# Attention's normed input, written by VectorE at the end of a step instead of by ScalarE at the start of the next

## The reference

```python
def _layernorm(x, axis=-1, eps=1e-05):
    m = jnp.mean(x, axis=axis, keepdims=True)
    v = jnp.var(x, axis=axis, keepdims=True)
    return (x - m) / jnp.sqrt(v + eps)
...
    h = _L0_tok_ref(x, ...)                        # out = einsum('bgcd,gbc->bcd', x, softmax weights)
    h = h + _L0_attn_ref(_layernorm(h, axis=-1), ...)
    h = h + _L0_ffn_ref(_layernorm(h, axis=-1), ...)
```

## Time and profile before

| | |
|---|---|
| median of 3 runs | 495.94 us (493.77 to 498.94) |
| profiled execution, its own time | 495.68 us |
| its span, first to last instruction | 493.5 us |
| PE busy | 428.6 us (87%) |
| DVE busy | 301.3 us (61%) |
| ACT busy | 250.2 us (51%) |
| POOL busy | 234.7 us (48%) |
| mean granted TensorE clock | 0.965 |

### The profile page before, as it was taken

How to read it: one execution, slowest core, us unless ns; L and a number is a source line. 1 busy time by engine, 2 the same in 40 slices (tenths; PEclk the granted TensorE clock), 3 DMA queues, 4 the chain that set the end, 5 groups by cost and what they waited for, 6 DMA issues and landing times.

```text
span 493.5 us, 13284 instructions
## 1 busy us (share of the span) xinstructions
PE 428.6 (87%) x3982; PEld 332.6 (67%) x3982; DVE 301.3 (61%) x1045; ACT 250.2 (51%) x708; POOL 234.7 (48%) x267
## 2 busy tenths in 40 slices
PE   1568889999999999766479999999999999978985
PEld 1546667777777777532368887888888888863654
DVE  3674678999899887875514344444443434341997
ACT  4165687887788876543025444444454544430000
POOL 1060003566556667667606556565665656560000
PEclk9989999999999999997679999999999999998998
DMA  8999990122122122222246596677677757635995
GB/s 265 344 352 263 291 278 30 68 80 86 68 75 69 66 77 89 80 83 94 101 131 209 161 294 204 182 237 215 187 237 216 244 139 218 213 132 208 405 393 211
DMA packets 56479, 90.01 MB, mean 182 GB/s; under 512 B 7720, under 2 KB 43691, under 8 KB 56401
## 3 DMA queue, kind: packets, MB, share of 16 engines
q1 hardware_dynamic: 44016, 61.69, 41.1%
q0 software_dynamic: 10080, 25.29, 14.5%
q10 hardware_dynamic: 2304, 2.10, 1.2%
HBM read 84.00 MB, written 40.82 MB: 253 GB/s over the span
## 4 chain that ended last, share of the span: by engine, by line
PE 35%; issue 7%; POOL 3%; DMA 2%; DVE 2%; SPq 1%; POOLq 0%; DVEq 0%
PE ps_low L1104 19%; PE ps L1104 11%; PE ps_low L1356 4%; POOL y_rows L449 3%; PE ps L1343 2%; DMA y_rows<-y,xring 1%; DMA xring<-slot_rows 1%; DVE x_sb L862 0%; DVE h_all L1087 0%; POOL slot_rows L420 0%; DVE x_sb L1099 0%; DVE x_sb L1092 0%; SPq L302 0%; SPq L352 0%; SPq L357 0%
## 5 line engine op out<-in xcount | busy, mean ns | idle before, releaser
L449 POOL DMA_INDIRECT y_rows<-y,xring x114 | 112.1, 983 | 90.1 <-issue 81.6
L1104 PE MATMUL ps_low<-wring,probt 128*128 x456 | 118.7, 383 | 0.0
L1065 DVE TENSOR_TENSOR probt<-probt,ps_low 128x128 f32<-128x128 f32 x114 | 32.8, 288 | 107.2 <-issue 92.6
L1104 PEld LDWEIGHTS ps_low<-wring,probt 128*128 128x128 f32 x456 | 78.6, 193 | 6.2
L1104 PE MATMUL ps<-wring,probt 128*128 x228 | 68.2, 382 | 0.0
L600 ACT COPY probt<-ps_low 128x256 f32<-128x256 f32 x115 | 42.8, 372 | 48.8 <-PE ps_low L1356 48.7
L605 ACT ACTIVATE probt<-ps_low 128x128 f32<-128x128 f32 x114 | 31.6, 277 | 57.3 <-PE ps_low L1104 57.3
L1058 DVE TENSOR_SCALAR y<-ps,xring 128x256 f32<-128x256 f32 x114 | 54.6, 479 | 7.2 <-DMA y_rows<-y,xring 6.0
L420 POOL DMA_INDIRECT slot_rows<-row,slot_ix x48 | 48.7, 1014 | 16.9 <-issue 16.9
L420 POOL DMA_INDIRECT slot_rows<-xring,slot_ix x48 | 47.2, 983 | 15.6 <-issue 15.3
L386 POOL TENSOR_TENSOR rs<-rv,minus_half 128x2 f32<-128x2 f32 (+1 forms) x20 | 13.1, 656 | 78.0 <-DVE nm L739 78.0
(11 more groups left out here) (200 smaller groups left out, 745.4 us busy)
## 6 DMA issues: line engine op xcount, KB each, us to landing
wring<-wexp SPq DMA_DIRECT2D x115, 384.0 KB
xring<-slot_rows SPq DMA_DIRECT2D x115, 129.0 KB, 2.8
x_sb<-y_rows SPq DMA_DIRECT2D x16, 768.0 KB, 6.8
slot_rows<-pads SPq DMA_DIRECT2D x1, 8256.0 KB, 36.6
x_sb<-x SPq DMA_DIRECT2D x3, 2048.0 KB, 17.8
slot_rows<-pads SPq DMA_DIRECT2D x5, 516.0 KB, 9.6
x_sb<-x SPq DMA_DIRECT2D x4, 512.0 KB, 5.3
out<-h_all ACTq DMA_DIRECT2D x16, 128.0 KB, 5.4
```

The costliest lines, as they stand in the source:

```text
L449: nc.gpsimd.indirect_dma_start(out=y_dram, out_offset=bass.IndirectOffsetOnAxis(ap=xring[:, q, TO_AT:TO_AT + 1].bitcast(I32), axis=0), in_ ...
L1065: nc.vector.tensor_tensor(hm[:, t % 2, :], silu[:, t % 2, :], psS[t % 2][:, INTER:2 * INTER], ALU.mult).then_inc(S("h_ready"), 1)
L1104: return nc.tensor.matmul(*a, **k)
```

## The change

ACT's operation goes. DVE writes the same values as the last operation of its routing part, one step earlier in the numbering of the loop (DVE's step b writes image b+3, which was ACT's work in step b+1). DVE waits for the root of the same step (`root_ready` at b+4), which POOL starts from the `rv` and `nm` that DVE wrote a few instructions before. It takes the mean from `mv`, so it uses `rs` but not `mrs`. PE's and POOL's instructions stay as they are.

```diff
@@ ScalarE, step(b, par) @@
-                if has(a) and a >= 2:
-                    act.wait_ge(S("root_ready"), b + 3)
-                    wait(act, S("xn_transposed"), a - 1)
-                    nc.scalar.activation(xn[:, par, :], h_all[:, a, :], ACT.Identity, bias=mrs[:, q, 0:1],
-                                         scale=rs[:, q, 0:1]).then_inc(S("ln1_done"), 1)
@@ VectorE, step(b, par), behind the last routing operation @@
                 for k in range(8, ROUTE):
                     routed(k)
+                if has(a):
+                    dve.wait_ge(S("root_ready"), b + 4)
+                    wait(dve, S("xn_transposed"), a - 1)
+                    nc.vector.tensor_scalar(xn[:, q, :], image(h_all, a), mv[:, 0, 0:1], rs[:, par, 0:1],
+                                            ALU.subtract, ALU.mult).then_inc(S("ln1_done"), 1)
                 if b in PART_AT:
                     gelu(PART_AT[b])
```

## The result

The changed kernel takes 503.43 us (median of 4 runs, 502.89 to 505.25), the kernel before 497.26 us in its runs beside it (4 runs, 493.77 to 498.94): the estimated ratio is 1.0145, its 95% interval 1.0096 to 1.0194 (the estimate, here and below, is not exactly the quotient of the two medians, which is 1.0124). The profiled execution of the change took 502.89 us, against 495.68 before and the 502.3 of the forecast. A second set of runs gave 500.94 against 494.21, a ratio of 1.0117 (1.0070 to 1.0164). By these estimates the change costs 1.2 to 1.5%; the two intervals reach from 0.7 to 1.9%.

What follows compares the result with a forecast made beforehand. PE and ACT were taken to set mid-loop steps by a few tenths of a microsecond, with DVE right behind. Terms 2.18 + 1.54 + 1.38 + 1.48 = 6.58 us on 495.68 gave 502.3 us; 8-in-10 range 497.2 to 505.6.

Steps and rivals of the forecast that it cites:

- The delay of the mixes: End of DVE's step: first mix starts 1.68 us behind `rv` instead of 0.59, so 1.09 us later, mostly standing for POOL.
- What lies beside a wait: Loop steps lose 1.09 us less their slack: 5 and 9 2.18, 6 and 11 1.54, 7, 10 and 12 1.38 us.
- Steps 4 and 8: They begin behind a `gelu` waiting for ACT's tanh, which covers the delay: nothing; without cover up to 0.73 us each.
- Step 13: Like steps 2 and 3, its slack before nmax is above 1.09 us, so it costs nothing.
- ACT's gain at nothing: ACT loses a 0.67 us operation in 14 steps; nmax to the shift's copy stays 4.04 us, so it gains nothing.
- The start-up: Step 0: DVE stands until POOL's `mrs` ends at 34.61 us; nmax comes at 35.76, 1.48 us late.
- the upper bound: 505.6 us: adds 1.5 for a longer `mrs` and 1.8 for a low-clock stretch on PE in step 0.
- ScalarE bounds the step: Rival: seven steps in which ACT also sums images each end up to 0.67 us earlier, 491.0 us; chance 0.05.
- the step gives it back: Rival: PE or ACT catch up later in the chain; 497.2 us, or 499.7 with half given back; chance 0.22.
- POOL did not come later: Rival: POOL's scatters drift ahead of its root in seven steps, adding 8.8 us, 511 us; chance 0.04.
- a delay at the last scatter reaches the end whole: Loop's end: experts' tiles wait for POOL's last scatters, which start some 6.6 us later, so DVE's delay reaches the end whole.
- the prediction's estimate from the Trainium skill: The moved operation on DVE takes 0.19 us by the page's rule instead of 0.41; the sum would be 5.5, so 501.2 us.

Runs made afterwards that it cites:

- the wait alone: The kernel before, with only DVE's wait for POOL's root added at the end of its step, ACT still writing `xn`: 500.12 us, ratio 1.0083.
- the operation moved away from the wait: The change, with DVE's write of `xn` moved behind the next step's first two mixes, ahead of nmax: 498.1 us, ratio 1.0054 against the kernel before.
- the three pairs: Three profiles of the kernel before set against three of the change: nmax of 4 to 13 grew by 4.52, 4.52 and 4.48 us.
- the kernel with two images on DVE: The kernel before, with DVE writing `xn` of images 4 and 5 alone and ACT the others: 493.75 us, ratio 0.9959.
- `rs` alone: The change, with DVE waiting only for `rs` and not for `mrs` behind it: 499.58 us, ratio 1.0080 against the kernel before.
- image 2 on ACT: The change, but ACT writes `xn` of image 2, the first of the loop: 499.9 us, ratio 1.0096 against the kernel before.
- no `xn`: The kernel before without ACT's write; nobody writes `xn` of images 2 to 15, so tokens route otherwise: 504.89 us, ratio 1.0169.
- PE's scores first: The kernel before, with PE making the next image's scores ahead of this image's weighted sum of V: 508.2 us, ratio 1.0272.

## Why the prediction was right, point by point

The time came out as forecast, and the main cause, a DVE that stands for POOL ahead of its mixes, is the one that was forecast. The match of the sum, 6.58 us against the 6.2 between the medians, is in part luck: in the loop it was 1.0 to 1.5 us too high (5.10 against 3.64 to 4.12 from nmax 2 to 13), and start-up and end made that up.

**The delay of the mixes** was read right to the hundredth: 1.32 + 0.04 + 0.32 = 1.68 us behind `rv`, measured 1.68, with 0.69 us of idle time for POOL and 0.41 for the operation. The two runs that take one part away each show that both parts count: the wait alone costs 3.15 us from nmax 4 to 13, the operation moved away from the wait 0.94 without the low-clock stretch, both together 4.52.

**What lies beside a wait** was mis-sized, 5.10 for 4.49 us in seven steps. Steps 5 and 9 cost 1.13 and 1.06 (forecast 1.09 each); 7, 10 and 12 cost 0.43, 0.39 and 0.43 (0.46); but 6 and 11 only 0.52 and 0.53 (0.77). Two things were missed. The slack is not the bracket alone: in step 6 before, nmax started 1.20 us behind the first mix, 0.41 more than the 0.79 of a step without slack, while the bracket said 0.32, because DVE's instructions overlap by some 0.08 us. And `rv` itself came earlier than before in those steps, 8.71 us behind nmax instead of 8.87, since a wait of 0.16 us for `mv` went. In 7, 10 and 12 the slack was 0.71 or 0.72 by the starts, not 0.63, and `rv` came 0.01 to 0.06 us later: two small errors that partly cancel. Steps 6, 7 and 10 to 12 all come out at 11.17 to 11.19 us, whatever they took before, so that the cost of a step that becomes DVE-bound is this length less its old one.

**Steps 4 and 8**, covered by the `gelu`, cost nothing, as forecast: the first mix is 2.19 us behind `rv` in both kernels in step 4. Step 13 cost 0.16, with no account of it.

**ACT's gain at nothing** was wrong in step 2. I compared nmax to the shift in steps 5 and 10, and took it for all; but it is not 4.04 us in each step, and in step 2 it was 5.19, where ACT had no idle time up to `vaug`. The size is -0.41 to -0.49 us in the three pairs, and the kernel with two images on DVE shows it as well, with ACT's rows. Step 3 was shorter too in some pairs, but it varies in the kernel before (12.30 to 12.67), so nothing follows.

**The start-up** was right in its first part and missed its second. DVE stands for POOL's root as forecast, and nmax of step 0 follows at 35.36, 35.47 and 35.62 us in the three profiles of the change (forecast 35.76). How much later that is depends on the kernel before, which has it at 34.28, 35.60 and 35.41: 1.08 us later, 0.13 earlier, 0.21 later, for the forecast 1.48. Behind it step 0 takes 1.91, 1.50 and 1.50 us longer, in a stretch at a granted clock of 0.50, which I had put into the upper bound alone. Up to nmax of step 2 the pairs then differ by +3.45, -0.16 and +1.71 us; that the term lies among these is luck.

What brings the clock down in step 0 stays open. In six profiles (three of the change, the wait alone, `rs` alone, image 2 on ACT) PE stood 1.79 to 2.20 us in one piece there, the clock fell at 37.4 to 40.2 us, and step 0 took 15.25 to 16.81 us. In six others (three of before, `xn` behind the mixes, no `xn`, two images) PE stood 0.74 to 1.39 us, the clock didn't fall there, the projection took 2.05 us, and step 0 13.75 to 14.20. With PE's scores first, in another order of PE, it stood 1.39 us, and the clock didn't fall there either. But the same wait a little later goes without a fall. The third profile of the change has this row, and one with 1.81 us at 52.78; that of the kernel before has 1.81 us at 51.07; in both the clock then stayed at 1.00 up to 60 us:

```profile
47.20 0.91 PE L1104 MATMUL ps<-gel,w_sb 32*128 32x4 f32 x7 [1.90 <-DVE gel L678]
```

No run changed the wait in step 0 alone, so it is a coincidence at one place and not a cause that is shown.

**The rivals.** That ScalarE bounds the step holds for step 2 alone. That the step gives it back does not hold: 4.04 us from nmax to the shift in steps 5, 9 to 13 of both kernels. POOL did not come later: it idled 2.12 us or more before its root in each of steps 4 to 12. That a delay at the last scatter reaches the end whole fits the first pair (+6.89, then +0.2) and is not shown by the others (+3.1, -2.0). The experts' stage shows no loss beyond these variations.

## What to carry to other kernels

Before an operation moves to another engine, count the wait that it brings along: here the engine's stand for GpSimd's root cost twice what the operation did, and of the two repairs tried for all 14 images the one that gave more back, by the estimates, was a place in the queue at which the awaited value is nearly ready. Read slack step by step, and as a distance between starts, not as an average and not from the bracket alone; a step pays only from the point where the new owner becomes last. An operation need not move as a whole: moving it for image 4, for which the giver was late and the taker had time, is what gained half a microsecond, while the loop's loss came from seven others.

## What the runs showed of the hardware

**GpSimd's short operation waits for VectorE's mix.** In 15 roots of the loop in the kernel before (third profile) `mrs` took 0.19 or 0.20 us nine times and 0.38 to 0.42 six times; in the change 0.19 or 0.20 all 15 times. The six long ones all run beside the second mix of a step and end 0.05 or 0.06 us behind it; none of the nine short ones runs beside that operation. With `xn` behind the mixes the long one is back, here POOL and then DVE:

```profile
119.81 0.38 POOL L389 TENSOR_TENSOR mrs<-nm,rs 128x2 f32<-128x2 f32 x1
```

```profile
119.66 0.48 DVE L724 SCALAR_TENSOR_TENSOR h_all<-x_sb,wtok,h_all 128x256 f32<-128x256 f32 x1
```

It ends at 120.19, 0.05 us behind the mix (120.14). That mix reads two tensors. Beside `xn`, which reads one, `mrs` kept its 0.19 us (at 120.16 in the kernel that waits for `rs`, `xn` from 120.12 to 120.54). The Trainium skill, "SBUF — State Buffer", section "SBUF: two separate sides", has a port pair that VectorE and GpSimd lock in turn, VectorE with two SBUF inputs or in a two-port mode; the rows agree, and show no such lock by `xn`. By that, `xn` would not run in a two-port mode here, which would also explain why it takes 0.41 us and a slot of 0.33 and not the 0.19 of the prediction's estimate from the Trainium skill; no run shows that by itself.

**The start-up's clock.** The same kernel's start-up differs by up to 3.75 us from one execution to the next, by stretches of 3 to 7 us at a granted clock of 0.50 that come at 28 to 35 us and, in some, again at 47 to 59 us. A difference of under 1% between two single profiles says nothing until these are taken out.
